# One wait instead of two before the exponentials of a decoder stack on one core

## The reference

```
x = x + attention0(x, ctx)[0]                  # the same for every sample
x = x + mamba2(rms(x)) ; x = x + cross8(ln(x), ctx)   # 8 heads of 32
x = ln(x + causal16(x, x))                     # 16 heads of 16
x = ln(x + cross16(x, ctx))
x = ln(x + fc2(relu(fc1(x))))
x = ln(x + causal16(x, ctx))
x = x + down(gelu(up(x)))
each attention: softmax(q k^T) v,  softmax = exp(s - max(s)) / sum
```

## Time and profile before

| | |
|---|---|
| median of 3 executions | 1912.95 us (1910.57 to 1915.44) |
| the profiled execution | 1915.45 us |
| its span | 1913.6 us |
| busy: PE, PEld, DVE, ACT, POOL | 92%, 77%, 65%, 75%, 28% |
| chain that ended last, by engine | PE 77%, ACT 11%, DVE 8%, issue 3% |
| mean granted clock of TensorE | 0.97 of full speed |

### The profile page before, as it was taken

The page is one execution under the profiler, slowest core; times in us unless marked ns, Lnnn a source line. Parts: engine busy times, 40 slices in busy tenths (PEclk is TensorE's granted clock), DMA queues, the critical chain, the costliest instruction groups (busy, mean ns, idle before and its releaser), DMA issues.

```text
span 1913.6 us, 49793 instructions
## 1 busy us (share of the span) xinstructions
PE 1763.0 (92%) x18768; PEld 1478.5 (77%) x18768; DVE 1242.4 (65%) x3163; ACT 1430.5 (75%) x4218; POOL 531.6 (28%) x1288
## 2 busy tenths in 40 slices
PE   5688999999999999999999999999999999999876
PEld 4467788887887888878788888878888878788764
DVE  2356767766667676666767666667676666767532
ACT  3256778878777887877778887777887877778653
POOL 1223223332232333223223323232333223232100
PEclk7689999999999999999999999999999999999987
DMA  6000000000000000000000000000000000000000
GB/s 238 6 7 7 10 10 5 7 10 10 10 10 10 10 2 10 10 10 10 10 10 2 10 10 10 10 10 10 10 2 10 10 10 10 7 8 2 4 4 6
DMA packets 26156, 26.60 MB, mean 14 GB/s; under 512 B 2240, under 2 KB 25024, under 8 KB 25792
## 3 DMA queue, kind: packets, MB, share of 16 engines
q1 hardware_dynamic: 25920, 23.41, 3.8%
HBM read 19.21 MB, written 4.19 MB: 12 GB/s over the span
## 4 chain that ended last, share of the span: by engine, by line
PE 77%; ACT 11%; DVE 8%; issue 3%; POOL 0%; DMA 0%; DVEq 0%; SPq 0%; ACTq 0%; POOLq 0%
PE ring L491 23%; PE ring L497 20%; PE ring L485 15%; PE score L547 6%; PE output L589 5%; ACT exps L860 5%; PE ring L674 3%; DVE rec L1201 3%; ACT L860 2%; PE output L579 2%; DVE neg_max L1054 1%; PE score L538 1%; ACT K L970 1%; ACT attT L872 1%; ACT decay L924 1%
## 5 line engine op out<-in xcount | busy, mean ns | idle before, releaser
L860 ACT ACTIVATE exps<-score,neg_max 128x128 f32<-128x128 f32 x1808 | 494.3, 403 | 91.7 <-DVE neg_max L1054 91.3
L1054 DVE TENSOR_REDUCE neg_max<-score 128x4 f32<-128x512 f32 x452 | 290.0, 684 | 48.0 <-PE score L547 44.9
L1305 POOL TENSOR_TENSOR stat<-stat 128x1 f32<-128x1 f32 x224 | 129.7, 582 | 678.1 <-DVE stat L1026 666.7
L485 PE MATMUL ring<-const,exps 128*128 128x128 f32 x1808 | 261.1, 282 | 34.5 <-ACT decay L924 20.2
L485 PEld LDWEIGHTS ring<-const,exps 128*128 128x128 f32 x1808 | 201.8, 143 | 79.7 <-ACT exps L860 37.5
L866 ACT COPY weights<-ring 128x512 f32<-128x512 f32 x452 | 251.5, 596 | 11.2 <-PE ring L485 5.2
L1138 DVE SCALAR_TENSOR_TENSOR conv<-raw,vectors,conv 128x128 f32<-128x128 f32 x576 | 169.1, 349 | 6.7
L491 PE MATMUL ring<-actT,w_q 128*128 128x128 f32 x1024 | 138.0, 279 | 0.9 <-ACT actT L829 0.9
L547 PE MATMUL score<-K,QB 32*128 32x128 f32 x3616 | 134.5, 282 | 1.9 <-ACT exps L860 1.7
L829 ACT COPY actT<-ring 128x256 f32<-128x256 f32 x224 | 89.4, 399 | 58.9 <-PE ring L485 58.8
L547 PEld LDWEIGHTS score<-K,QB 32*128 32x128 f32 x3616 | 113.4, 187 | 21.1 <-issue 15.6
(11 more groups left out here) (163 smaller groups left out, 3548.3 us busy)
## 6 DMA issues: line engine op xcount, KB each, us to landing
cT<-in_ctxT SPq DMA_DIRECT2D x32, 128.0 KB, 2.3
x_in<-in_x SPq DMA_DIRECT2D x32, 128.0 KB, 2.2
out<-result SPq DMA_DIRECT2D x32, 128.0 KB, 1.7
row_all<-in_rows SPq DMA_DIRECT2D x1, 1420.0 KB, 9.8
w_in<-in_in_proj SPq DMA_DIRECT2D x1, 1288.0 KB, 7.2
w_k<-in_k SPq DMA_DIRECT2D x4, 256.0 KB, 5.2
w_v<-in_v SPq DMA_DIRECT2D x4, 256.0 KB, 5.3
w_q<-in_q SPq DMA_DIRECT2D x4, 256.0 KB, 5.6
```

What stands on the lines that cost most here:

```text
L485: last = nc.tensor.transpose(t[:, c * P:(c + 1) * P], src[:, c * P:(c + 1) * P], ident)
L860: last = run(exps[:, n, h * P:(h + 1) * P], of, ACT.Exp, bias=neg_max[:, m, h:h + 1])
L1054: nc.vector.tensor_reduce(neg_max[:, m, 4 * half:4 * half + 4].rearrange("p (b h) -> p b h", b=each), score[:, first:first + each, 0:4 // ...
L1305: tt(stat[:, l, 10:11], stat[:, l, 2:3], stat[:, l, 4:5], ALU.pow).then_inc(S[done], 1)
```

## The change

The exponentials no longer wait for the second half of the turn two parts before. In its place an assertion, evaluated when the program is built, says that on ScalarE that turn's task stands ahead of the exponentials' task; turned_out, in that task, waits for the same semaphore.

```
@@ for n, (a_, t, l, i) in enumerate(SLOTS):
     if n >= WEIGHT_BUFFERS:
         before(SLOTS, n, WEIGHT_BUFFERS, lambda a_, t, l, i: (f"values{a_}", l, i), turn_task)
+    if n >= EXPS_BUFFERS:
+        old = SLOTS[n - EXPS_BUFFERS]
+        assert PLACE_OF["ACT"][turn_task(*old)] < PLACE_OF["ACT"][f"scores{a_}_{t}", l, i], (old, a_, t, l, i)
@@ def exponential(it, a_, l, t):
                 n, m = buffer(it, a_, l, t, EXPS_BUFFERS), buffer(it, a_, l, t, MAXIMA_BUFFERS)
-                earlier = earlier_part(it, a_, l, t, EXPS_BUFFERS) if a_ else None
-                if earlier:
-                    filled(earlier[0], *turn_job(*earlier[1:], 1))
                 for half in range(HALVES):
                     act.wait_ge(S["maxima"], part(it, a_, l, t) * HALVES + half + 1)
```

## The result

Four executions of the changed kernel took 1879.75 to 1881.97 us, median 1880.34, against 1913.23 for the kernel before (four executions): 0.983 of it, 95% interval 0.9813 to 0.9847. That is 32.9 us less; the forecast was 1884 us with 29.1 us less and a range of 1878 to 1893. The profiled execution took 1881.97 us, its span is 1880.1 us, 33.5 us shorter than that of before.

A forecast was written before the change was run, and what follows sets the result against it. The prediction took TensorE to bound the kernel, with table loads behind VectorE's maxima in its chain. Terms of 24.9, 2.7 and 1.5 us summed to 29.1, giving 1884 us from the median 1912.95, range 1878 to 1893.

The forecast's parts named there:

- What bounds the kernel: Mostly TensorE; some 38 us of the chain is "ACT L860", table loads behind VectorE's maxima, costing TensorE 20.2 us of pauses.
- The load leaves the chain: At scores2_0 on ScalarE the load ends 0.53 us ahead of the maximum, so the exponentials start 1.33 us earlier.
- 0.86 us of the 1.33 reach TensorE: Turn of scores2_0 starts 0.86 us earlier, held by the flip x4T; 29 samples give 24.9 us.
- modelled pause (0.70): TensorE's profiled pause before the turn of scores2_0, counted from the flip's modelled end; using it takes off 4.6 us.
- The 30th and 31st load: Loads at 1815.05 and 1884.97, TensorE having nothing else to do: whole 1.33 us each, 2.7 us; lower bound 1.7.
- What is late next: Behind the turn, the copy of x4T and VectorE's line 1175 are ready in time, with 0.3 and 0.7 us to spare.
- The separate waits: Before scores4_0 one costs some 0.05 us, 1.5 us over 30 samples; the other 163 or so taken as nothing, at most 8.2.
- The sum: 24.9 + 2.7 + 1.5 = 29.1 us less, 1884 us against the median; this case has 84%.
- No drain ahead of the load: Rival: ScalarE must drain before loading the table, so the gain is 21.3 us and the time 1892; 3%.
- The load does not wait: Rival: the load is still held behind the maxima, leaving 1.5 to 3 us, 1910 to 1911.5; 3%.
- in the 15 us behind the turn TensorE has no new pause: Rival: a later wait takes the place in the sample, so the gain is 12.9 us and the time 1900; 8%.
- the clock stayed at 1.00: Rival: with fewer pauses TensorE's clock falls in the steady part and the kernel is slower, 1919 or more; 2%.

The follow-up runs named there:

- four more: Changed kernel with four idle activations added on ScalarE between the copy of V2 and the load of scores2_0: 1890.91 us, 0.9884 of the kernel before.
- exchanged waits: Kernel before with the two waits ahead of the exponentials in the other source order, both kept: 1879.48 us, 0.9832 of the kernel before.
- two more: Changed kernel with two idle activations added on ScalarE between the copy of V2 and the load of scores2_0: 1879.49 us, 0.9824 of the kernel before.
- wait at scores2_0 alone: Kernel before with the second wait kept only at scores2_0, the other 192 separate waits gone: 1906.6 us, 0.9968 of the kernel before.
- first edit: Changed kernel with att_full0 to 3 made one semaphore that counts to four: 1873.82 us, 0.9792 of the kernel before.
- both edits: Changed kernel with att_full0 to 3 as one counting semaphore and VectorE's maxima no longer waiting for earlier exponentials: 1869.57 us, 0.978 of the kernel before.
- wait everywhere else: Kernel before with the second wait kept everywhere but at scores2_0, 192 separate waits staying: 1884.34 us, 0.9857 of the kernel before.
- six more: Changed kernel with six idle activations added on ScalarE between the copy of V2 and the load of scores2_0: 1913.87 us, 1.0 of the kernel before.

## Why the prediction was right

- *What bounds the kernel.* The entry "ACT L860" of the chain was the place; it is gone from the chain, and the pauses for the decays (20.2 us, 29 times) are gone from the waits of TensorE.
- *The load leaves the chain.* Right in place and size: it starts where the copy of V2 ends, with 0.56 us left to the maximum, where 0.53 was worked out. It was hidden by ScalarE's wait for VectorE; the run with four more activations shows what happens when that cover is used up.
- *0.86 us of the 1.33 reach TensorE.* The turn gained 0.87, and the slack of 0.46 or 0.47 was found in three kernels. Taking the difference of starts (0.86) and not the modelled pause (0.70) was right. The step left out the turn's second half, which uses the bank of the second decay: 0.07 us a sample, 2 us in all.
- *The 30th and 31st load.* Half wrong. For "TensorE has nothing else to do" the prediction gave ScalarE's idle time before the loads, which doesn't tell it. At the 30th the flip stands ahead of the turn, and 0.74 us came out and not 1.33. At the 31st it is the full 1.33: from the start of that part's scores to its turn TensorE has 4.88 us before and 3.55 after. That makes 2.1 us for the term instead of 2.7, inside its bounds of 1.7 and 2.7.
- *What is late next.* The copy of x4T and line 1175 held, as reckoned. Line 1175 has 0.4 us to spare and not 0.7: the decay pair takes 1.37 us instead of 1.13. Its second half starts at 864.5, where TensorE's decay matmuls end (862.56 + 1.96 = 864.52), so it waits for its matmul, as far as a modelled end can tell.
- *The separate waits.* 0.06 us at attT, where 0.05 was put. I took nothing for the others for want of a row; the kernel with the exchanged waits has 224 that are over already, and a sample as long as without them.
- *The sum.* 29.1 us, or 30.5 with the 0.07 added in 29 samples and 2.1 for the last two loads, against 32.9 measured. The two traces, 33.5 us apart, divide it. Up to the 29th exponentials behind a load they differ by 28.9 us, where 26.4 was forecast and 28.4 with the 0.07. From the 29th load to the 30th it took 57.3 us before and 53.3 after, 3 us more of a gain than a steady sample's, at a mean granted clock of 0.94 and 1.00; the last stretch, from the exponentials behind the 31st load on, took 27.3 us before and 28.7 after, at 0.81 and 0.76. The 3 us go with the clock and not with the table load, as the same stretch in the other kernels shows (the table below). The forecast had no term for this. So the mechanism was right and its size nearly so, and that the total came within 4 us owes something to chance: what the clock takes or gives in the last 150 us is as large as the terms that were left out.
- *The rivals.* No drain ahead of the load, 0.02 us between the copy of V2 and the load, and none behind it: before the change the exponentials start 0.02 us after the load's end (874.67 and 874.69). The Trainium skill (ScalarE: Activation LUTs, "What ACT_TABLE_LOAD costs") gives 1283 ns and some 1380 ns of drain; this case's traces agree on the first and show none of the second. The load does not wait; in the 15 us behind the turn TensorE has no new pause; the clock stayed at 1.00 from 200 to 1700 us.

The stretches behind these clocks, by the windows of the trace (stretch and length, busy PE, PEld, DVE, ACT, POOL with counts, clock, DMA share, GB/s), first of the kernel before:

```profile
1757.74:1815.05 57.31, 50.36 (x544) 42.06 (x541) 31.05 (x74) 39.08 (x113) 6.83 (x15) 0.94 0.01 4
1886.26:1913.60 27.34, 15.92 (x102) 12.88 (x102) 3.92 (x11) 10.68 (x31) 1.46 (x3) 0.81 0.02 6
```

then of the changed kernel:

```profile
200.00:1700.00 1500.00, 1465.27 (x16094) 1241.37 (x16093) 1064.65 (x2712) 1228.97 (x3614) 456.22 (x1102) 1.00 0.03 9
...
1728.31:1781.57 53.26, 47.44 (x549) 40.09 (x553) 31.02 (x73) 39.03 (x113) 8.18 (x15) 1.00 0.02 4
...
1851.44:1880.10 28.66, 16.29 (x104) 12.97 (x102) 5.26 (x13) 10.69 (x31) 1.47 (x3) 0.76 0.02 5
```

Over the ten traces of this study, from the start of the 29th load of line 860 (865 in some) to that of the 30th:

| mean granted clock in the stretch | kernels | longer than the same kernel's median sample by |
|---|---|---|
| 1.00 | changed, two more, wait at scores2_0 alone, first edit, both edits | -1.01 to -0.95 us |
| 0.97 | waits exchanged, four more | 0.58 and 0.59 us |
| 0.94 | before, wait everywhere else, six more | 1.92 to 2.07 us |

Of the kernels at 0.94 one has the load behind the maxima and two have it ahead; of those at 1.00 one has it behind and four ahead. So what this stretch takes doesn't hang on the load. What decides which clock a kernel gets there isn't shown.

## What to carry to other kernels

An instruction that the build puts in front of another (here a table load) takes its place among the waits that the source gives: look in the order of instructions at whether it stands behind a wait that it doesn't need, and give the instruction behind it one wait only, or put first in the source the wait that should be its own. The gain here was not the instruction's length but what the next engine in line has no other reason to wait for; read it from the starts of the two instructions there, and ask what stands between them. Once the pauses are small, waits that end last and are instructions of their own are worth counting: several semaphores that are always awaited together can be one that counts.

## What the runs showed that I had not expected

With two waits ahead of one activation, in both orders that were built, the one that comes last in the source became an instruction of its own, and the first stayed with the activation; exchanging two lines, which changes nothing in what is waited for, gave 34.5 us (1879.48 against 1914.01). A separate wait costs some 0.06 us when it ends last (2.64 against 2.58 us of idle time before scores4_0) and nothing that a sample's length shows (54.27 against 54.27 us) when it is over before. And 0.14 and 0.17 us per sample, far below what one would look at in a profile, went with 4.3 and 6.5 us less over 32 samples.
